# Four landing buffers instead of two, and loads issued across block borders, for the mixed weight of layer 1

## The reference

```python
# layer 1, gated branch; K = 8 adapters picked from 32, each W is 1024 x 1024, float32
Wsel = W[ids]                                   # (8, 1024, 1024)
bsel = b[ids]
out = jnp.einsum('k,kod,bsd->bso', weights, Wsel, x)
out = out + jnp.einsum('k,ko->o', weights, bsel)
g = silu(out)
x = x + s * g                                   # s: attention with q, k, v, o projections of the same xn
```

## Time and profile before

| What | us |
|---|---|
| Median of two runs | 3346.71 (3316.56 and 3376.86) |
| The profiled execution, own time | 3270.64 |
| Its span on the slowest core (core 4) | 3269.1 |
| Spans of the eight cores | 3248.2 to 3269.1 |
| Granted TensorE clock, mean over a core's span | 0.778 to 0.780 |
| Drain, from its first matmul to its last | 2381.5 to 2486.8 |

### The profile page before, as it was taken

How to read it: one execution, slowest core, us unless ns; L and a number is a source line. 1 busy time by engine, 2 the same in 40 slices (tenths; PEclk the granted TensorE clock), 3 DMA queues, 4 the chain that set the end, 5 groups by cost and what they waited for, 6 DMA issues and landing times.

```text
span 3269.1 us, 39748 instructions; the slowest of 8 cores (3248.2 to 3269.1 us)
## 1 busy us (share of the span) xinstructions
PE 2322.0 (71%) x15302; PEld 1265.0 (39%) x15302; DVE 878.9 (27%) x1693; ACT 860.6 (26%) x1189; POOL 80.1 (2%) x152
## 2 busy tenths in 40 slices
PE   1399999994676556886777776176766565887877
PEld 0144444432233223564655664154554221332333
DVE  1544444442222264432222112400100000112122
ACT  2111111102111155554444443011100223222222
POOL 0000001100000000000000000000000000000000
PEclk9699999997887765655556556598898885988888
DMA  4222222202111010101001001523142102011010
GB/s 118 29 30 30 30 30 37 35 4 55 16 17 17 9 44 1 59 8 52 2 5 56 2 2 34 179 65 78 49 148 75 26 0 52 1 52 52 1 52 26
DMA packets 58442, 128.65 MB, mean 39 GB/s; under 512 B 7561, under 2 KB 15755, under 8 KB 55700
## 3 DMA queue, kind: packets, MB, share of 16 engines
q1 hardware_dynamic: 33364, 90.46, 8.3%
q0 software_dynamic: 24896, 35.66, 7.2%
HBM read 142.88 MB, written 18.88 MB: 49 GB/s over the span
## 4 chain that ended last, share of the span: by engine, by line
PE 56%; ACT 16%; DVE 13%; issue 7%; DMA 6%; DVEq 1%; ACTq 0%; SPq 0%; POOL 0%; PEldq 0%; POOLq 0%
PE PS L885 8%; PE PS L719 6%; ACT EB L907 6%; PE PS L1189 5%; PE PS L591 5%; PE PS L600 5%; PE PS L1332 4%; PE PS L1401 4%; PE PS L634 4%; PE PS L1161 3%; PE PS L1272 2%; ACT PRJ L727 2%; DVE PS L890 2%; DMA PLAND<-Wsel 2%; DVE ACC L645 1%
## 5 line engine op out<-in xcount | busy, mean ns | idle before, releaser
L885 PE MATMUL PS<-Q,K 64*128 64x128 bf16 x2176 | 274.2, 304 | 124.9 <-ACT EB L907 119.8
L907 ACT ACTIVATE EB<-PS,negBh 128x1152 bf16<-128x1152 f32 (+7 forms) x128 | 204.0, 1594 | 257.7 <-DVE PS L890 242.8
L885 PEld LDWEIGHTS PS<-Q,K 64*128 64x128 bf16 x2176 | 211.7, 135 | 154.2 <-issue 143.5
L1161 PE MATMUL PS<-identw,PLAND 128*128 128x128 f32 x1024 | 147.9, 309 | 125.8 <-DMA PLAND<-Wsel 96.4
L634 PE MATMUL PS<-HT,WDT 128*128 128x512 bf16 x768 | 197.6, 394 | 34.8 <-DVE HT L617 21.9
L1189 PE MATMUL PS<-XN,W1FULL 128*128 128x512 bf16 x768 | 179.8, 395 | 58.9 <-ACT Q L1204 18.6
L719 PE MATMUL PS<-XN,WBLK 128*128 128x512 bf16 x768 | 210.4, 442 | 10.1 <-DVE K L734 5.1
L890 DVE TENSOR_TENSOR PS<-PS,trinegT 128x128 f32<-128x128 f32 x256 | 76.6, 300 | 439.9 <-PE PS L885 431.7
L1161 PEld LDWEIGHTS PS<-identw,PLAND 128*128 128x128 f32 x1024 | 140.5, 222 | 135.3 <-issue 135.1
L591 PE MATMUL PS<-XN,WGT 128*128 128x512 bf16 x768 | 172.2, 383 | 7.3 <-DVE ACC L645 5.6
L600 PE MATMUL PS<-XN,WUT 128*128 128x512 bf16 x768 | 169.7, 379 | 0.0
(11 more groups left out here) (160 smaller groups left out, 2527.3 us busy)
## 6 DMA issues: line engine op xcount, KB each, us to landing
PLAND<-Wsel SPq DMA_DIRECT2D x64, 512.0 KB, 3.5
XF<-xT SPq DMA_DIRECT2D x1, 8192.0 KB, 38.3
XT<-xT SPq DMA_DIRECT2D x4, 2048.0 KB, 8.2
x1park<-XT SPq DMA_DIRECT2D x32, 256.0 KB
X1CH<-x1park SPq DMA_DIRECT2D x8, 1024.0 KB, 8.3
XT<-x1park SPq DMA_DIRECT2D x4, 2048.0 KB, 8.2
outT<-XT SPq DMA_DIRECT2D x32, 256.0 KB
LAND<-wg POOLq DMA_DIRECT2D x16, 256.0 KB, 4.2
```

The lines of the kernel that those rows point to most:

```text
L885: tS = P.op("tensor", lambda t, h=h, gi=gi, tt=tt, off=off: t.matmul(PS[:, off + tt * 128:off + (tt + 1) * 128], head_k(h, ts(tt, 128)), h ...
L907: s.activation(EB2[:, slot, 0:klen], PS[:, 0:klen], AF.Exp, bias=negBh[:, h:h + 1]), inc=True)
L1161: li=li: t.matmul(BK(bki, jj * 128, (jj + 1) * 128), PLAND32[:, li, ts(u, 128)], identw8[:, k, :], start=(k == 0 and u % 4 == 0), stop=(k ...
```

## The change

The landing buffer has four slots instead of two, with four semaphores. The tiles are numbered through, `gu = oc * 8 + k` from 0 to 63, and slot and semaphore are `gu % 4`. Four loads are issued before the first step. Behind step `gu` the load of tile `gu + 4` is issued, also when it belongs to the next block. `identw8` moves up by 8 KB. Matmuls, copies, their waits for each other, and the number and size of the loads are as before.

```diff
     DMA_SEMS = ("dc", "dx", "dx2", "dst", "dl0", "dl1", "dl2", "dl3",
-                "dr0", "dr1", "dr2", "dr3", "dw", "dp0", "dp1")
+                "dr0", "dr1", "dr2", "dr3", "dw", "dp0", "dp1", "dp2",
+                "dp3")
...
-    PLAND32 = ar.place("PLAND32", [128, 2, D], F32, oG)
-    identw8 = ar.place("identw8", [128, 8, 128], F32, oG + (8 << 10))
+    PLAND32 = ar.place("PLAND32", [128, 4, D], F32, oG)
+    identw8 = ar.place("identw8", [128, 8, 128], F32, oG + (16 << 10))
...
     def premix_gen():
-        pl_guard = {0: None, 1: None}
+        pl_guard = {0: None, 1: None, 2: None, 3: None}
         prev_ev = None
         dm_toks = {}
 
-        def issue(oc, k):
-            li = k % 2
+        def issue(gu):
+            li = gu % 4
             P.wait("sync", pl_guard[li])
-            dm_toks[k] = P.dma("sync", PLAND32[:, li, :],
-                               Wsel_d[k, oc * 128:(oc + 1) * 128, :],
-                               sem=f"dp{li}")
+            dm_toks[gu] = P.dma("sync", PLAND32[:, li, :],
+                                Wsel_d[gu % 8, (gu // 8) * 128:
+                                       (gu // 8 + 1) * 128, :],
+                                sem=f"dp{li}")
+        for gu0 in range(4):
+            issue(gu0)
         for oc in range(EC):
-            issue(oc, 0)
-            issue(oc, 1)
             tT = None
             for k in range(8):
-                li = k % 2
-                P.wait("tensor", dm_toks[k])
+                gu = oc * 8 + k
+                li = gu % 4
+                P.wait("tensor", dm_toks[gu])
...
                 pl_guard[li] = tT
-                if k + 2 < 8:
-                    issue(oc, k + 2)
+                if gu + 4 < 64:
+                    issue(gu + 4)
                 yield
```

## The result

The changed kernel takes 3238.5 us (median of 12 runs) against 3269.1 us for the kernel before (median of 11 runs): 0.990 of it, 95% interval 0.987 to 0.993, or about 32 us less (the difference of the two medians is 30.6). Some executions of either kernel show one half of the chip, or both, at a lower clock and take 1.5 to 6% more, and the ratios here leave them out. The two runs shown ahead of the prediction, 3316.56 and 3376.86 us, are among the four highest of eleven.

The account below looks back on a forecast made before the run. The drain was taken as bound by too few tiles in flight, not by DMA rate; -29.1 + 2.7 - 1.1 + 0.3 = -27.2 us, against the median 3346.7 gives 3319.5 us, range 3270 to 3350.

Parts of the forecast that it names:

- part 1: Drain of the premix: four slots remove all 25 waits for tiles, 29.1 us less, with no wait remaining.
- the two ways to price it: Drain gain either from step prices, 30.6 us less, or from taking out only the counted waits, 29.1 us, which was taken.
- The sum by step prices: Drain built from a slow first step, 34 steps of 1.905 us and four block borders: 74.7 us, 30.6 us less.
- Part 2: Start of the K pass: two more tiles beside its weight's load make that load 2.7 us longer.
- Part 3: Start of the V pass: one tile fewer beside its weight's load, a gain of 1.1 us.
- Part 4: The rest: pass loads stay hidden, two more semaphores cost 0.3 us at barriers, later code moves forward by the whole gain.
- The sum: Whole kernel: -29.1 + 2.7 - 1.1 + 0.3 = -27.2 us, 3243.4 from the profiled execution or 3319.5 from the median.
- B: Drain: more tiles in flight bring no more than 170 GB/s, only 2.4 us less there; kernel 3346 us; chance 0.06.
- the forecast's own case: Whole kernel: the terms hold as summed, 29.5 to 23.5 us less, 3317 to 3323 us; chance 0.72.
- A: Drain: loads become the bound at 2.39 us a tile, 23.8 us less instead of 29.1; kernel 3324.8; chance 0.11.
- C: Drain: denser float32 matmuls are granted less clock; at 1.2 GHz it takes 18.6 us more, kernel 3367; chance 0.05.
- D: K and V passes: clocks of the mixed-in steps may fall otherwise, 5 us either way; chance 0.06 of going beyond.

Follow-up runs that it names:

- two slots across blocks: Changed kernel with two slots again, loads still numbered through and issued across block borders: 3267.5 us, ratio 0.998 to the kernel before.
- after: The changed kernel itself, four slots and four semaphores, against the kernel before: 3238.5 us, ratio 0.990; 3236.8 us in the profiled execution.
- held tiles: Changed kernel with SP held, so the additional tiles load only after the K pass's weight has landed: 3226.2 us in one execution.
- doubled loads: Changed kernel with every tile from number 29 on loaded a second time into a buffer nobody reads: drain 106.2 us in one execution.
- early weights: Changed kernel with layer 1's K, V and Q projection weights each loaded a stage earlier: 3185.7 us, ratio 0.975 to the kernel before.
- late extra: Changed kernel meant to load two additional tiles only behind step 2, but all four left at once: 3227.8 us in the profiled execution.
- delay: Changed kernel with the bias load done twice on SP's queue ahead of the gate pass: code behind the premix 648.2 us.
- early weights and tiles: Changed kernel with the three projection weights loaded a stage earlier and the first four tiles loaded in the layer norm: ratio 0.979, 3198.8 us profiled.
- the last experiment on the kernel before: Kernel before, two semaphores, plus two idle waits on every engine ahead of both premix barriers: 3259.2 us in one execution.

## Why the prediction was right in its parts and wrong as a number

**What bounds the kernel, and part 1: right in the mechanism, a little low in size.** The waits of the drain fell from 23.9 us (median core) to nothing, its length by 30.6 us. Core 4, from which I had read, went from 105.3 to 71.5, 33.8 us less where I had 29.1 to 30.6; all cores lie under the 73 to 79 us that I gave for the drain (71.3 to 72.4). The loads kept up, with a share of 0.70 (0.68 foretold) at 227 GB/s (217), and no wait remained. Of the two ways to price it I took the worse. Taking out the counted waits gives 23.9 us on the median core, and 6.7 are missing. A wait costs more than its idle time. One step alone, behind a wait, takes 2.02 us; eight that run on take 14.53 (core 1 of after, the timeline as in the earlier trace rows):

```profile
2390.96 14.53 PE L1164 MATMUL PS<-identw,PLAND 128*128 128x128 f32 x128 [1.48 <-DVE WMIXT L1174]
```

So a further step adds (14.53 - 2.02) / 7 = 1.79 us, and a run of steps that breaks off costs 0.23 us on top of its idle time, the tail of its last records. Some 26 breaks make 6.1 of the 6.7 us. The sum by step prices, 74.7 us for the whole drain, was within 3 us of the 71.8 measured. It was too high because I took 1.905 us a step from pairs, in which half a tail is counted with each step, while a long run has 1.82 to 1.84.

**Part 2: right, a little low.** +3.3 us (core 4: 22.8 us, where I gave 21.5 to 22.3), where I took 2.7 from the landing times and had 3.1 from the engine time. The held tiles show the cause. The engine time of the tiles is the nearer price here, where the engines are full.

**Part 3: right in its direction.** -1.5 us on the median core, near the engine time's figure; I took 1.1. Core 4 has 15.1 us, where I gave 14.4 to 14.9. Since this load varies from 16.0 to 16.9 us among kernels that have the same tiles beside it, the size isn't better known than 0.8 to 1.7.

**Part 4: the term for the semaphores was mis-sized and had the wrong sign.** I priced two more waits at a barrier at 0.3 us for their issue. That cost can't be seen: from the drain's last matmul, over the barrier, to the gate pass's first evacuation it is 22.7 us before and after. But with them the untouched code behind got 6.3 us faster, and waits alone did the same. That the code behind the drain "moves forward by the whole gain" held; that it then takes as long as before did not. By themselves drain and loads give 28.8 us of the 31 to 32.

**The sum** was -27.2; measured are -31.0 on the median core and a ratio of 0.990, -32 us. That is outside the forecast's own -29.5 to -23.5, and the parts that it did price come to -28.8. The rest, -6.3 behind and some -2 in the two passes against +5.3 ahead of all changed code, it did not have; that these largely cancel, and leave the total as near the sum as it is, is luck. The predicted ratio, 3243.4 to 3270.6 or 0.992, lies in the measured interval. Against the profiled execution's own time the sum gives 3243.4 us; 3238.5 was measured, and 3236.8 in the profiled execution.

**The step that failed is the last one,** "Against the median the sum is 3319.5, and this is what I give", and with it the range from 3270. I had two levels, 3270.6 for the one execution I could look into and 3346.7 for the median of two that lay 1.8% apart, and let the second carry the number. All rows and all terms of the sum came from the first, whose eight cores stood between 3248.2 and 3269.1 us at granted clocks of 0.778 to 0.780; two runs 60 us apart, 1.4 and 3.2% above it, were no evidence for a level of 3347. Eleven runs put the kernel before at 3269.1, and the changed kernel came at 3238.5, 81 us under the 3319.5 given, while the change itself was 0.010 where 0.008 was given. I wrote that the range "takes B above and most of the spread below", and then ended it at 3270, which is the profiled time before any gain: the forecast's own case, on the level that the profile showed, lay outside it.

**The rivals.** A falls by the doubled loads: 1.65 us a tile. B falls with it; the DMA engines had room. C: in the denser drain the granted clock was 0.98 with the slow first step in the window, and 0.98 over the drain before with its own slow first step, so denser float32 matmuls weren't granted less. By the Trainium skill, "TensorE: Matmul & The Clock Gate", section "Seeing it yourself", which says to budget 1.95 GHz for sustained dense matmuls on all cores, a step would by my estimate have taken 2.34 us. It took 1.84, and the trace disagrees here as in the feed-forward. D was the one that mattered: untouched stages moved by 6.3 us, just beyond its 5, for which I had 0.06. I had looked for it in the K and V passes (some 2 us there) and not in the 650 us behind.

## What to carry to other kernels

At DMA shares of 0.53 to 0.70 the number of buffers in flight was a matter of latency here: a tile must be asked for one landing ahead, counted in steps at full speed, and the landing to count with is the longer one under the new load (3.5 us became 4.6). Price what remains by the rate of the engine that will bound the stretch, taken from its longest run without a break, not by taking counted idle time out, and look at what else is loading when the deeper prefetch starts, since that is where it costs. Hang the predicted time on the execution whose trace carries the argument, and when two levels of time are shown, ask first which of them that trace belongs to.

## What the runs showed of the hardware that I had not expected

The time of code that nobody touched moved with waits elsewhere that wait for nothing. From the Q pass's first evacuation to the end the same instructions took mostly 648, 655, 658 or 662 us. In most of the traced executions five to eight of the eight cores show the same time, though they come to this code up to 24 us apart, each counted from its own start; the kernel before, with 651 to 661, is the exception. Each row is one traced execution of each kernel:

| Kernel | behind, median of cores | spans, median of cores |
|---|---|---|
| two semaphores (before; two slots across blocks) | 654.5; 655.9 | 3256.3; 3258.4 |
| two semaphores and four idle waits on every queue | 647.7 | 3247.9 |
| four semaphores, two slots | 647.7 | 3249.2 |
| four semaphores, four slots (four kernels without the early weights that keep this code: after, late extra, held, delay) | 647.8 to 648.2 | 3213.9 to 3225.3 |
| three slots, three semaphores | 661.5 | 3241.2 |
| double loads | 658.3 | 3267.4 |
| early weights; early weights and tiles | 648.0; 658.3 | 3178.4; 3188.6 |

Where I looked, two kernels differ in the clock granted to TensorE in single rounds of the attention, in which it stops and starts every few microseconds. Waits alone brought the change once (the last experiment on the kernel before), and one or two on TensorE's queue or a delay of some 2 us did not on most cores. It isn't the chip: the levels 648, 655.9, 658.3 and 661.5 all came up on one and the same chip. How the waits act, and on which queue, stays open: whether by where later instructions lie when they are fetched, or by a shift of the engines against each other that the barriers don't remove, no run here tells apart. The size is what to keep in mind: 6.8 us of 3260 by a handful of waits, and up to 14 us between kernels in which this code is the same, nearly half of the gain of this case. A comparison of whole kernel times alone would have read it as an effect of the edit; the table by stages did not.

The other numbers: with eight cores loading 512 KB tiles a core gets 318 GB/s at a DMA share of 0.96, 1.65 us a tile; a landing of 3.5 us with at most two tiles under way becomes 4.6 with four slots and 10 to 12 when the engines are full.
